# Layer one's local convolution by pairs of heads, with a placing transfer, in a two-layer kernel on one core

## The chip, the core and the metric

One NeuronCore of a Trainium2 chip runs the whole program. The metric is device time in microseconds of that core, the median of several runs. Engines run their own instruction streams and meet only at semaphores: TensorE (PE; PEld is its weight load), VectorE (DVE), ScalarE (ACT), GpSimd (POOL) and SyncE (SP, which here only issues DMAs).

## The reference

16 batches of 1024 tokens and 256 features pass through two layers. Layer zero (a retention with an MLP, then a mixture of experts) is not touched. Layer one is a local dynamic convolution and an MLP. Its convolution, cut to what matters (16 heads of 16 features, a window of 31 tokens):

```python
avg = jnp.cumsum(x, axis=1) / jnp.arange(1, l + 1)[None, :, None]
ci = avg.reshape(b, l, H, d).transpose(0, 2, 1, 3).reshape(b * H, l, d)
pc = ci @ W_pe + b_pe
energy = stt + jax.nn.sigmoid(pc[..., K:]) * pc[..., :K]
w = jax.nn.softmax(energy, axis=-1)              # one kernel of 31 weights for each token and head
for kk in range(K):
    out = out + w[:, :, kk:kk + 1] * padded[:, kk:kk + l, :]
v = conv_loc @ W_fc.T + residual                 # conv_loc: out with the heads side by side
v = (v - mu) / jnp.sqrt(var + EPS) * gamma + beta
```

Around it stand x + ga * v, layer norms with a scale and shift by batch, and an MLP with ReLU (256 to 1024 to 256).

## The kernel before

Layer one runs from about 1941 us to the end of the span. It goes over 16 batches, each cut in 16 slots of a plan. In every slot PE does one slice of the MLP: `l1_expand` (L2294, six matmuls, 512 columns each) and `l1_contract` (L2308, twelve matmuls of 256 columns), of an earlier batch. Between them it does the attention of the current batch: `turn_in` and `turn_mid` (transposes, L130), `kernel_product` (the energies, L2239 and L2244), `window_turn` (transposes, L130), `convolve` (L2265) and `mix` (L2274, L2276).

The order on each engine is written out by the tables `PLACES_D` (batches 2 to 15) and `STARTS_D` (batches 0 and 1): each step has a place in slots, `order_d` turns the places into a plan, all batches' plans are merged by place (batch b starts at slot 16 b) and every engine walks the merged list `t.steps` and issues its own part of each step, in that order. `BANKS_D` says how long a step keeps a PSUM bank; `timed_banks` hands out the banks by it. One batch in the middle of the layer is 16 slots on every engine.

The convolution in blocks of TT = 96 tokens, 11 in a batch (NT), 176 in all:

- `softmax`: DVE makes the 31 weights of each token and head (tile w), and SP writes them to a matrix in DRAM, `bands`, along its diagonals (L1877).
- `load_band`: SP reads the block's matrix back as `bandT` [128 input tokens, 96 output tokens, 16 heads] (L1847, two transfers). The heads are innermost, so one head's 96 columns stand 16 elements (64 bytes) apart.
- `window_turn`: PE turns 128 tokens of the averages, and ACT copies them to `window` (L2022), which has for every pair of heads two 32-column stationary tiles, each with one head's 16 columns and 16 columns of zeros (set once by POOL, L1954 and L1955).
- `convolve`: for each half of the features (k), for odd and even, for four column groups g of 32, one matmul with a 32-column stationary tile and 96 moving columns of bandT. The four g write to partitions 32g to 32g + 31. The odd matmul adds to the even one in PSUM, which the zeros make right. That is 16 matmul calls in a block; each fp32 call stands as two weight loads and two matmuls in the trace, so 32 of each. ACT copies 128x192 to `convT` (L2030), a circle of 384 tokens.
- `mix`: for each chunk of 128 tokens (8 in a batch), transposes of h3T and the product of convT with W_fc, into one bank.

POOL does `join` (moe rows times a gain row, L1935), `add_row` (L1943), the roots and the sum of `energies` (L1962). DVE needs that sum for `energies` (L2139, L2141) after it has made `gated` (L2133). `join` and `add_row` work on half a batch (four chunks, 128x1024) at a time.

## Time and profile before

| | us |
|---|---|
| three runs, median | 3465.27 |
| lowest, highest | 3462.51, 3465.64 |
| the profiled execution's own time | 3466.14 |
| its span | 3464.3 |

```profile
span 3464.3 us, 67597 instructions
PE 3307.4 (95%) x25168; PEld 2785.4 (80%) x25168; DVE 2606.8 (75%) x6172; ACT 2076.2 (60%) x4055; POOL 1269.7 (37%) x1073
PE   7999999999996999999999469999999999999999
DVE  5877887788777865555554578888888888888884
ACT  4677777777765555655665345555555555555554
POOL 1333333332331366666665332333333332322320
PEclk8999999999998999999999689999999999999999
PE 87%; DVE 6%; ACT 2%; DMA 2%; issue 1%; SPq 1%; POOL 1%; POOLq 0%; DVEq 0%; ACTq 0%
```

The second line gives each engine's busy time, its share of the span and its instructions. The digit rows cut the span in 40 slices of 87 us (9 is 90% or more busy); layer one is slices 23 to 40. PEclk is the granted TensorE clock in tenths of full speed. The last line is the chain of work that ended last, followed back and summed by engine.

### The profile page before, as it was taken

To read this page: it belongs to the slowest core of one execution; us is meant where nothing else is said; L and a number is where in the kernel's file an instruction comes from. 1 tells how busy PE (TensorE), PEld (TensorE's weight loads), DVE (VectorE), ACT (ScalarE), POOL (GpSimd) and SP (SyncE) were. 2 spreads that over 40 slices of the span, in tenths; PEclk is the share of its full clock that TensorE was granted. 3 is DMA by queue.
4 is the path that set the end of the run, shared out by engine and by line. 5 is a ranking of instruction groups with operands and counts; after the bars stand their busy time and mean duration, and the time that the engine had idled before them with its cause. 6 is when DMAs were issued, how large, how long until landed. Compare 5 with 4: busy or idle time off the path is not lost.

```text
span 3464.3 us, 67597 instructions
## 1 busy us (share of the span) xinstructions
PE 3307.4 (95%) x25168; PEld 2785.4 (80%) x25168; DVE 2606.8 (75%) x6172; ACT 2076.2 (60%) x4055; POOL 1269.7 (37%) x1073
## 2 busy tenths in 40 slices
PE   7999999999996999999999469999999999999999
PEld 4888888888885799999999347888888888888888
DVE  5877887788777865555554578888888888888884
ACT  4677777777765555655665345555555555555554
POOL 1333333332331366666665332333333332322320
PEclk8999999999998999999999689999999999999999
DMA  5332233222212344444444465555655555655541
GB/s 180 102 114 90 93 114 108 80 64 80 75 45 80 87 115 103 96 104 109 105 97 86 86 132 113 113 127 127 129 125 127 120 123 126 130 125 128 128 102 41
DMA packets 746021, 366.38 MB, mean 106 GB/s; under 512 B 551278, under 2 KB 696246, under 8 KB 745558
## 3 DMA queue, kind: packets, MB, share of 16 engines
q1 hardware_dynamic: 717278, 319.57, 36.4%
q0 software_dynamic: 28416, 42.49, 6.6%
q8 instruction: 201, 3.29, 0.4%
q14 instruction: 126, 1.03, 0.1%
HBM read 224.93 MB, written 135.99 MB: 104 GB/s over the span
## 4 chain that ended last, share of the span: by engine, by line
PE 87%; DVE 6%; ACT 2%; DMA 2%; issue 1%; SPq 1%; POOL 1%; POOLq 0%; DVEq 0%; ACTq 0%
PE bank L2294 10%; PE bank L853 10%; PE bank L1612 10%; PE bank L2308 10%; PE bank L1596 10%; PE bank L833 10%; PE bank L2265 7%; PE bank L130 5%; PE bank L810 3%; PE bank L2244 3%; PE bank L2276 3%; PE bank L2239 1%; ACT sides L1140 1%; PE bank L818 1%; PE bank L846 1%
## 5 line engine op out<-in xcount | busy, mean ns | idle before, releaser
L1492 DVE TENSOR_TENSOR hidden_low<-bank,hidden_high 128x512 fp32r<-128x512 f32 x256 | 176.2, 689 | 263.0 <-ACT hidden_high L1193 262.8
L609 ACT ACTIVATE bank<-bank,b 128x512 f32<-128x512 f32 x256 | 172.7, 675 | 282.2 <-PE bank L833 281.9
L1186 ACT ACTIVATE bank<-bank,fc_bias 128x512 f32<-128x512 f32 x256 | 169.5, 662 | 263.5 <-PE bank L1596 263.5
L853 PE MATMUL bank<-w_high,gT_low 128*128 128x256 f32 x1024 | 309.8, 303 | 2.9 <-DVE gT_low L725 2.9
L2052 ACT ACTIVATE bank<-bank,l_b 128x512 f32<-128x512 f32 x256 | 168.9, 660 | 238.8 <-PE bank L2294 238.8
L2308 PE MATMUL bank<-l_w_high,l_hidden_low 128*128 128x256 f32 x1024 | 307.6, 300 | 0.0
L2265 PE MATMUL bank<-bandT,window 128*32 128x96 f32 x5632 | 271.2, 345 | 22.4 <-DMA bandT<-bands 20.2
L853 PE MATMUL bank<-w_low,gT_high 128*128 128x256 f32 x1024 | 289.4, 283 | 0.0
L853 PE MATMUL bank<-w_high,gT_high 128*128 128x256 f32 x1024 | 289.4, 283 | 0.0
L2308 PE MATMUL bank<-l_w_low,l_hidden_high 128*128 128x256 f32 x1024 | 286.0, 279 | 0.0
L2308 PE MATMUL bank<-l_w_high,l_hidden_high 128*128 128x256 f32 x1024 | 285.5, 279 | 0.0
L2265 PEld LDWEIGHTS bank<-bandT,window 128*32 128x32 f32 x5632 | 187.8, 124 | 90.3 <-issue 46.0
L725 DVE TENSOR_TENSOR gT_low<-bank,gT_high 128x512 fp32r<-128x512 f32 x256 | 172.9, 685 | 113.4 <-ACT gT_high L616 113.4
L1962 POOL TENSOR_TENSOR energies<-energies,energy 128x496 f32<-128x496 f32 x128 | 162.0, 1266 | 209.3 <-DVE energies L2133 209.3
L1106 POOL DMA_INDIRECT moe_output<-ys,idx x128 | 212.3, 1659 | 70.5 <-issue 55.1
L2294 PE MATMUL bank<-h4T_high,l_w_low 128*128 128x512 f32 x512 | 223.2, 436 | 6.8 <-DVE l_v L2166 6.7
L853 PEld LDWEIGHTS bank<-w_high,gT_low 128*128 128x128 f32 x1024 | 194.8, 190 | 24.0 <-issue 13.1
L2308 PEld LDWEIGHTS bank<-l_w_high,l_hidden_low 128*128 128x128 f32 x1024 | 192.6, 188 | 23.4 <-issue 18.9
L833 PE MATMUL bank<-hT_high,w_low 128*128 128x512 f32 x512 | 204.2, 399 | 2.3 <-POOL hT_low L536 2.3
L853 PEld LDWEIGHTS bank<-w_low,gT_high 128*128 128x128 f32 x1024 | 195.5, 191 | 12.0 <-issue 7.2
L833 PE MATMUL bank<-hT_low,w_high 128*128 128x512 f32 x512 | 203.7, 398 | 0.0
L2294 PE MATMUL bank<-h4T_high,l_w_high 128*128 128x512 f32 x512 | 203.0, 396 | 0.0
(372 smaller groups left out, 10709.3 us busy)
## 6 DMA issues: line engine op xcount, KB each, us to landing
bandT<-bands SPq DMA_DIRECT2D x352, 240.0 KB, 3.7
fc_full<-in_L_ffn_fc_wT SPq DMA_DIRECT2D x32, 1024.0 KB, 5.5
bands<-zeros SPq DMA_DIRECT2D x22, 768.0 KB, 8.6
x<-in_L_attn_x SPq DMA_DIRECT2D x32, 512.0 KB, 6.3
moe_output<-zeros SPq DMA_DIRECT2D x32, 512.0 KB, 7.1
x_after_retention<-x SPq DMA_DIRECT2D x32, 512.0 KB, 2.9
moe_input_and_gates<-xn SPq DMA_DIRECT2D x32, 512.0 KB, 7.7
moe<-moe_output SPq DMA_DIRECT2D x32, 512.0 KB, 7.4
```

What stands on the lines that cost most here:

```text
L130: t = pe.transpose(bank[:, i * rows:(i + 1) * rows], source(i), ident[0:rows, 0:rows])
L609: e.activation(bank[:, :], bank[:, :], ACT.Gelu_apprx_tanh, bias=t.b1[:, f:f + 1]).then_inc(s("g_full"), 1)
L725: v.tensor_tensor(t.gT.low[:, f % SLICES, :], K.banks[t.bank["expand", i, f, 0]][:, :], t.gT.high[:, f % SLICES, :], ALU.subtract).then_in ...
L833: m = pe.matmul(bank[:, :], w, h, start=k + j == 0, stop=k == KD - 1 and j == 2)
L853: m = pe.matmul(out, x, w, start=False, stop=f == KF - 1 and j == 2 and c % 2 == 1)
L1106: e.indirect_dma_start(K.moe_dram, bass.IndirectOffsetOnAxis(ap=t.idx[i % 4][:, n:n + 1], axis=0), t.ys[i % 2][:, n, :], None, compute_op= ...
L1492: v.tensor_tensor(t.hidden.low[:, n % SLICES, :], K.banks[t.bank["expand", i, f, 0]][:, :], t.hidden.high[:, n % SLICES, :], ALU.subtract) ...
L1596: m = pe.matmul(bank[:, :], w, y, start=k + j == 0, stop=k == KD - 1 and j == 2)
L1612: p = pe.matmul(y_chunk(K, ch), y, w, start=first and j == 0, stop=f == KF - 1 and j == 2 and ch % 2 == 1)
L2265: m = pe.matmul(bank[32 * g:32 * (g + 1), k * TT:(k + 1) * TT], t.window[n % 2][:, pair, odd, :], t.bandT[n % 2][:, :, g // 2 * H // 2 + k ...
L2294: m = pe.matmul(bank[:, :], w, x, start=k + j == 0, stop=k == KD - 1 and j == 2)
L2308: p = pe.matmul(K.banks[6 + ch // 2][:, left:left + D], x, w, start=False, stop=f == KF - 1 and j == 2 and ch % 2 == 1)
```

## The change

- `window` has one 32-column tile for a pair of heads instead of two with zeros; its columns alternate between the two heads (d, q). ACT's copy L2022 writes with a step of two. The zeroing by POOL and its event go.
- `convolve` has one matmul for a pair of heads, k and g as before: 8 calls instead of 16. The moving side is bandT's columns of both heads, 96 x 2 = 192 columns, pairs of neighbouring elements that stand 64 bytes apart. Each row of the product then holds its own head's result in every second column; the other columns are the other head's weights on this head's features and are not used.
- ACT takes the product with two copies: all 128 rows of the odd columns to a new tile `odd_heads`, all rows of the even columns to convT (128x192 each). A new step `place_odd` issues one DMA from ACT's queue that writes the odd rows of `odd_heads` over those of convT: 64 partitions, two runs of 384 bytes each for a full block.
- `mix` waits for the placing transfers of the last two blocks that it reads. Two blocks later, ACT waits for the transfer before it writes `odd_heads` again. The rows of W_fc are put into the same alternating order on the host.
- `join` and `add_row` become four steps of one chunk each (128x256). The semaphores `gained` and `x2r` count chunks, and all who wait for them do the same.
- All places of layer one and the times in `BANKS_D` are new.

```diff
-    t.window = K.ring(ctx, "window", 2, [P, H // 2, 2, 2 * t.HD])
+    t.window = K.ring(ctx, "window", 2, [P, H // 2, 2 * t.HD])
+    t.odd = K.ring(ctx, "odd_heads", 2, [P, KD, TT])
@@ pool
-            for k, cs in enumerate(pieces_of(n, HC)):
-                e.wait_ge(s("shared"), halves_done(n) if n else k + 1)
-                e.tensor_tensor(t.moe[n % 2][:, cs, :], t.moe[n % 2][:, cs, :], t.row_in[:, :].unsqueeze(1).to_broadcast([P, cs.stop - cs.start, D]),
-                                ALU.mult).then_inc(s("gained"), 1)
+            e.wait_ge(s("shared"), halves_done(n) if n else k // 2 + 1)
+            e.tensor_tensor(t.moe[n % 2][:, k, :], t.moe[n % 2][:, k, :], t.row_in[:, :], ALU.mult).then_inc(s("gained"), 1)
...
-            e.tensor_tensor(x2[:, :, :], x2[:, :, :], t.row_bias[:, :].unsqueeze(1).to_broadcast([P, HC, D]), ALU.add).then_inc(s("x2r"), 1)
+            e.tensor_tensor(x2[:, k, :], x2[:, k, :], t.row_bias[:, :], ALU.add).then_inc(s("x2r"), 1)
@@ scalar
-            e.copy(out, src).then_inc(s("window"), 1)
+            e.copy(t.window[n % 2][:, :, :].rearrange("p a (d q) -> p a q d", q=2),
+                   K.banks[t.bank["window_turn", b, *args, 0]][:, 0:D].rearrange("p (a q d) -> p a q d", q=2, d=t.HD)).then_inc(s("window"), 1)
...
+            if n >= 2:
+                e.wait_ge(*K.later(f"odd_placed{n % 2}", 16 * (n // 2)))
+            heads = K.banks[t.bank["convolve", b, i, 0]][:, 0:2 * KD * TT].rearrange("p (k t q) -> p k t q", k=KD, q=2)
+            e.copy(t.odd[n % 2][:, :, 0:size], heads[:, :, 0:size, 1])
             if before:
                 e.wait_ge(s("mixed"), before)
-            e.copy(t.convT[:, :, place:place + size],
-                   K.banks[t.bank["convolve", b, i, 0]][:, 0:KD * TT].rearrange("p (k t) -> p k t", k=KD)[:, :, 0:size]).then_inc(s("convT"), 1)
+            e.copy(t.convT[:, :, place:place + size], heads[:, :, 0:size, 0]).then_inc(s("conv_taken"), 1)
+        elif name == "place_odd":
+            (i,) = args
+            n, size, place = b * NT + i, min(TT, K.S - i * TT), i * TT % t.CIRCLE
+            e.wait_ge(s("conv_taken"), n + 1)
+            e.dma_start(t.convT[1::2, :, place:place + size], t.odd[n % 2][1::2, :, 0:size]).then_inc(K.later(f"odd_placed{n % 2}")[0], 16)
@@ tensor
             for k in range(KD):
-                for odd in range(2):
-                    for g in range(4):
-                        pair = 4 * k + g
-                        m = pe.matmul(bank[32 * g:32 * (g + 1), k * TT:(k + 1) * TT], t.window[n % 2][:, pair, odd, :],
-                                      t.bandT[n % 2][:, :, g // 2 * H // 2 + k * t.HR + g % 2 * 2 + odd], start=odd == 0, stop=odd == 1)
+                for g in range(4):
+                    first = g // 2 * H // 2 + k * t.HR + g % 2 * 2
+                    out = bank[32 * g:32 * (g + 1), 2 * k * TT:2 * (k + 1) * TT].rearrange("p (t q) -> p t q", q=2)
+                    m = pe.matmul(out, t.window[n % 2][:, 4 * k + g, :], t.bandT[n % 2][:, :, first:first + 2], start=True, stop=True)
...
-            pe.wait_ge(s("convT"), NT * b + -(-(ch + 1) * P // TT))
+            last = NT * b + -(-(ch + 1) * P // TT) - 1
+            for n in range(max(last - 1, 0), last + 1):
+                pe.wait_ge(*K.later(f"odd_placed{n % 2}", 16 * (n // 2 + 1)))
```

The lines of `PLACES_D` of which the prediction speaks, before and after:

```diff
-    "kernel_product": (10.8, 12.8, 14.85, 16.8, 18.8, 20.8, 22.79, 24.8), "gated": (10.8, 12.8, 14.61, 16.8, 18.82, 20.8, 22.8, 24.8),
-    "energies": (11.61, 13.56, 15.61, 17.61, 19.47, 21.61, 23.61, 24.94),
-    "convolve": (16.82, 18.13, 19.59, 21.03, 22.48, 23.93, 25.38, 26.83, 28.28, 29.73, 31.18),
-    "mix": (19.06, 20.4, 21.9, 24.8, 26.2, 27.7, 30.6, 31.43), "center_mid": (19, 20.4, 21.9, 24.8, 26.21, 27.7, 30.6, 32),
+    "kernel_product": (10.8, 13.01, 14.91, 16.8, 18.93, 20.89, 22.77, 24.74),
+    "gated": (10.69, 12.36, 14.84, 16.96, 18.61, 20.81, 22.64, 24.58),
+    "energies": (11.36, 13.53, 15.74, 17.73, 19.27, 21.35, 23.56, 25.52),
+    "convolve": (16.97, 18.08, 19.67, 21.03, 22.22, 23.95, 25.04, 26.82, 28.62, 29.73, 31.18),
+    "place_odd": (17.09, 18.19, 19.9, 21.15, 22.42, 24.02, 25.25, 27.02, 28.74, 29.98, 31.32),
+    "mix": (19.15, 20.49, 22.1, 24.89, 26.55, 27.9, 31.23, 32.35),
```

## Rows read from the trace of the kernel before

**Rows 1.** Busy time by stretch: middle batches, then the layer's start.

```profile
core 0: us, PE busy (x) PEld busy (x) DVE busy (x) ACT busy (x) POOL busy (x), PEclk, DMA share, GB/s
2456.00:2546.00 90.00, 89.52 (x828) 73.26 (x826) 77.85 (x159) 52.34 (x107) 27.46 (x22) 1.00 0.58 125
...
2726.00:2816.00 90.00, 89.52 (x828) 73.49 (x826) 77.86 (x159) 52.54 (x106) 27.48 (x22) 1.00 0.59 125
...
1980.00:2070.00 90.00, 57.35 (x604) 41.10 (x604) 72.50 (x137) 38.47 (x80) 27.25 (x20) 0.78 0.67 137
```

**Rows 2.** Waits from 2456 to 2816 us (four batches): total, times, longest.

```profile
DVE top L2139 <- POOL energies L1962: 25.4, 24, 2.0
DVE energies L2133 <- ACT l_th L2002: 9.2, 12, 1.7
DVE total L2146 <- ACT energies L2010: 5.5, 8, 0.7
PE bank L2294 <- DVE l_v L2166: 1.9, 4, 0.5
```

**Rows 3.** Timeline of PE, 2700 to 2712 us: start, duration, instructions merged.

```profile
2700.73 1.53 PE L2265 MATMUL bank<-bandT,window 128*32 128x96 f32 x32
2702.19 0.50 PE L2294 MATMUL bank<-h4T_high,l_w_low 128*128 128x512 f32 x1
...
2703.69 0.28 PE L2308 MATMUL bank<-l_w_high,l_hidden_low 128*128 128x256 f32 x1
...
2705.19 0.49 PE L2239 MATMUL bank<-pe_bias,l_ones 64*128 64x496 f32 x2
...
2706.45 0.44 PE L130 MATMUL bank<-ident,avgT 128*128 128x128 f32 x2
2706.72 0.38 PE L2274 MATMUL bank<-ident,h3T 128*128 128x128 f32 x2
...
2710.72 0.74 PE L2304 MATMUL bank<-out_bias,l_ones 128*128 128x512 f32 x2
2711.30 0.28 PE L2308 MATMUL bank<-l_w_high,l_hidden_low 128*128 128x256 f32 x1
```

**Rows 4.** Lines from 2456 to 2816 us, shapes apart: busy, mean ns.

```profile
L2265 PE MATMUL bank<-bandT,window 128*32 128x96 f32 x1408 | 67.8, 344 | 0.0
L1962 POOL TENSOR_TENSOR energies<-energies,energy 128x496 f32<-128x496 f32 x32 | 40.1, 1254 | 39.7 <-DVE energies L2133 39.7
L1935 POOL TENSOR_TENSOR moe<-moe,row_in 128x1024 f32<-128x1024 f32 x8 | 20.5, 2565 | 39.2 <-ACT moe L1975 39.2
L2030 ACT COPY convT<-bank 128x192 f32<-128x192 f32 (+1 forms) x44 | 13.8, 314 | 22.1 <-PE bank L2265 22.1
```

**Rows 5.** Timeline of PE around the router's product in layer zero.

```profile
149.60 0.64 PE L867 MATMUL bank<-xnT,w_router 128*32 128x128 f32 x16
```

**Rows 6.** The router's product, all 512: duration min/median/max.

```profile
L867 PE MATMUL bank<-xnT,w_router x512: 272/273/421, 149.6 to 1074.2; 128*32 128x128 f32 x171
```

**Rows 7.** A convolution at low clock: PE's timeline, then its stretch.

```profile
1984.10 1.57 PE L2265 MATMUL bank<-bandT,window 128*32 128x96 f32 x32 [1.72 <-DMA bandT<-bands]
...
1984.00:1986.00 2.00, 1.57 (x32) 1.21 (x32) 1.97 (x3) 0.86 (x2) 0.00 (x0) 0.50 0.72 140
```

**Rows 8.** Timeline of ACT behind the convolution of Rows 3.

```profile
2702.34 0.32 ACT L2030 COPY convT<-bank 128x192 f32<-128x192 f32 x1 [0.69 <-PE bank L2265]
...
2704.59 0.59 ACT L2059 CAST l_hidden_high<-bank 128x512 fp32r<-128x512 f32 x1
```

**Rows 9.** Timeline of SP's queue: how long it is busy with an issue.

```profile
2702.33 0.77 SPq L1847 DMA_DIRECT2D bandT<-bands  x2
2705.90 0.32 SPq L1877 DMA_DIRECT2D bands<-w  x1
```

**Rows 10.** DMA issues: KB each, median us from issue to landing.

```profile
bands<-w SPq DMA_DIRECT2D x79, 62.0 KB, 4.2
...
ranks<-rank SPq DMA_DIRECT2D x4, 256.0 KB, 2.3
...
rows_layer<-rows SPq DMA_DIRECT2D x2, 64.0 KB, 1.9
...
x_after_retention<-x SPq DMA_DIRECT2D x32, 512.0 KB, 2.9
```

**Rows 11.** Waits from 1941 to 2070 us, the start of the layer.

```profile
PE bank L130 <- ACT moe L1982: 30.0, 2, 24.4
...
PE bank L2265 <- DMA bandT<-bands: 19.9, 6, 7.0
```

119 lines of the change are left out of this document (61 added, 58 removed).

## The prediction, made before the change was run

> **What bounds the kernel now.** I read the busy time by stretch first. In the middle of layer one a batch takes 90.0 us, and PE is busy 89.5 of them at full granted clock, while DVE is busy 77.9, ACT 52.3 and POOL 27.5 [rows 1]. Busy time of PE alone proves little, so the waits come next: over four batches PE waits 1.9 us for another engine, all else on the list are others waiting [rows 2]. PE's own stream therefore sets the 90 us, and what shortens that stream shortens the batch until DVE, with 77.9 us of work, becomes the limit. The chain that ended last gives PE 87%, which agrees. The layer's first 130 us are different: from 1980 to 2070 us PE is busy only 57 of 90 us, with waits of 30.0 us on ACT's moe and 19.9 us on bandT [rows 1, 11]. There latency sets the pace, and less work on PE brings little.
>
> **The convolution on PE.** A block of 32 matmuls lasts 1.53 us, one of them 0.344 us [rows 3, 4]. The four column groups run side by side, so 32 matmuls are eight steps of four, and the last start comes 1.53 - 0.34 = 1.19 us after the first: 1.19 / 7 = 0.17 us a step. The next line starts 1.46 us after the block's start. After the change there are 16 matmuls, four steps, each with 192 columns instead of 96. Everything hangs on the length of such a step.
>
> The router's product has the same form, 128x32 stationary, four column groups, fp32, but its moving columns stand side by side. Its 16 matmuls of 128 columns last 0.64 us at 0.273 each: (0.64 - 0.27) / 3 = 0.12 us a step [rows 5, 6]. So a step with four loads and four matmuls can be done in 0.12 us, and 128 columns cost less than the convolution's 96. Neither loads nor instructions set the 0.17 us, then, and by the router's 0.96 ns a column 96 columns would take 0.09. What differs is the 64-byte spacing of bandT's columns. A second row agrees: at the low level of the granted clock (0.50, 1.2 GHz) the block takes 1.57 us instead of 1.53 [rows 7, 3]; a step bound by the array would have doubled. I conclude that each separate place in bandT costs 0.17 / 96 = 1.8 ns whatever stands there. Then 96 places with a pair in each cost 0.17 us a step again, and 192 columns at the router's rate cost 192 x 0.96 = 0.18 us. The two ways agree on 0.17 to 0.18.
>
> The Trainium skill has two rules here that contradict each other. "TensorE: Matmul & The Clock Gate" (What happens when you issue a matmul) says that throughput is purely the number of columns streamed; 16 x 96 and 8 x 192 are the same number, and by that rule the saving is nil. "SBUF — State Buffer" (the note on cachelines) says that fp32 reads need two hits in a 16-byte line for full rate; by that rule pairs run at full rate and the step stays. The rows above speak for the second, and only for single elements; no row shows a pair.
>
> So a block gets four steps shorter: 4 x 0.17 = 0.68 us, or 7.5 us for the 11 blocks of a batch. Bounds: nothing, if a step of 192 takes 0.34 us, and 0.68 if it stays. In 15 batches (165 blocks) PE loses 165 x 0.68 = 112 us. In batch 0, where PE waits anyway, half the blocks run at the low clock, where 192 columns cannot be faster than the 1.2 GHz allows; I take nothing there.
>
> **ACT.** It gets a second copy, 0.31 us, and an issue of a DMA. No DMA is issued by ACT in this trace; SP's queue is busy 0.32 to 0.39 us with one [rows 4, 9]. That is 11 x (0.31 + 0.35) = 7.3 us a batch on an engine with 52.3 of 90 us: 59.6 of some 83. It stays second to DVE. A copy with a step of two on either side may be slower; at twice the 0.31 for both, another 7 us would still fit. Every copy, split or rectifier of ACT behind it comes up to 0.65 us later, and slots of the MLP have more than that between their parts (ACT now waits for PE before most of them).
>
> **The placing transfer and mix.** Before, mix could go 0.15 + 0.32 us after the convolution (PE's next line starts at 2702.19, the copy runs 2702.34 to 2702.66) [rows 3, 8]. Now: 0.15, two copies 0.63, in some blocks one `l1_split` of 0.59 ahead of the issue by the places (19.67 convolve, split of the slot, 19.9 place_odd), then the transfer. It moves 48 KB within SBUF, which no row shows. Nearest are the 64 KB and 256 KB issues with 1.9 and 2.3 us; 4.2 us for 62 KB into `bands` is the far end, with its many small runs, and 2.9 for 512 KB lies between [rows 10]. I take 2.3, near the small ones with some queueing. The sum is 3.1 us, 3.7 with the split, 5.6 at worst.
>
> What covers it is PE's work between convolution and mix, from the places: PE has an expand 1.50, a contract 1.50, an energies product 1.26 and a turn of the window 0.27 [rows 3]. Before, the chunk mixed at 27.7 had one contract and one turn behind its convolution (26.83), 1.8 us. In the new places the shortest are the chunks mixed at 20.49 and 27.9, behind the convolutions at 19.67 and 26.82: each has an expand, a turn and the first contract of a half between, which carries the output bias (0.58 us) [rows 3]: 3.8 us. The others have 4.1 us and more. The margin of the two is 0.1 to 0.7 us, so small delays on ACT or in the transfer will show; I charge 0.6 us a batch (ends: 0 and, at 5.6 us, 2 x 1.8 + 3 x 1.2 = 7 us). Behind a waiting mix stands the whole of PE, so each such wait counts in full.
>
> **POOL and DVE.** POOL's own time is the same but for a little overhead. Cutting a 2.57 us join into four lets the energies' sum (1.25 us) go after a chunk [rows 4]. DVE now waits 25.4 / 4 = 6.4 us a batch for that sum [rows 2], because in most chunks only one `l1_low` of some 0.7 us lies between `gated` and `energies` (places 10.8 and 11.61, 20.8 and 21.61). In the new places most chunks have more between (10.69 to 11.36 holds residual_mid and stats_x3; 12.36 to 13.53 an add_in besides), so I expect 1 to 2 us a batch to be left. That matters: DVE's 77.9 plus all its present waits of 12.1 is 90.0, and without relief DVE could not keep up with a batch of 82.5. With 2 us left, and 1.4 us for the exponentials' wait (5.5 / 4), it needs 81.3. That fits, with 1 us to spare, so some friction is to be expected; I charge 0.4 us a batch.
>
> **Start and end.** In batch 0 a mix has hardly cover, and five of eight could wait 2 us for the placing, partly inside the wait for bandT that follows: +3 us, between 0 and +10. POOL's zeroing that falls away is under 2 us at a time when PE waits for other things: nothing. The end behind the last convolution is the MLP's and stays.
>
> **Sum.** Profiled execution 3466.1 - 112 + 15 x (0.6 + 0.4) + 3 = 3372. It stands 0.9 us above the median of three, so 3371. A middle batch would be 90.0 - 7.5 + 1.0 = 83.5 us.
>
> **Rivals.**
> - Pairs cost double (slower). If each fp32 element read outside a contiguous run costs 1.8 ns, a step of 192 takes 0.34 us, PE's stream is as long as before, and the friction and the start remain: 3465 + 18 = 3483; with mix at its worse end, more. For it: the same number of elements is read, and no row shows a pair. Against: the element next door arrives with the same access if the limit is the place and not the element. The change turns slower once a step is above about 0.17 + 0.17 x (112 - 18) / 112 = 0.31 us. Chance 0.09.
> - DVE becomes the bound. If its waits for POOL and ACT stay at 7 to 9 us a batch instead of 3.4, a batch takes 85 to 87 us, and the time is 3465 - 15 x (3.0 to 5.0) + 3, some 3393 to 3423. For it: 94% load on an engine that waits in order. Against: the longer cover between its steps. Chance 0.13.
> - The placing transfer is late. With DMA engines busy 0.58 of the time [rows 1] it could land after 4.2 us; 7 us a batch would cost nearly all the gain. More likely 1.5 to 3.5 us a batch are lost beyond my charge: 3395 to 3425. Chance 0.05.
>
> **Chances and range.** The forecast (3371, its own range 3347 to 3392) has 0.73; the low end is the full 119 us with no friction. The range goes to 3422 to take in most of the next two. About 0.2% (7 us) is what a measurement tells here. Faster 0.89, same 0.02, slower 0.09.
>
> **What would show it.** L2265 has 2816 matmuls; a block lasts about 0.85 us (3 x 0.17 and one duration) instead of 1.53. If it lasts 1.3 or more, the first rival holds. A middle batch is 83 to 84 us with PE over 98% busy; PE waits for the placing DMA in front of L2274 show the third rival; PE waiting for l_hidden_low or bank readers on DVE, and DVE over 95% busy, the second. DVE's wait for L1962 should fall under 2 us a batch. ACT's busy time rises to about 56 us a batch, issues not counted.

## The result

| | us |
|---|---|
| the kernel before, 14 runs beside those of the changed one, median | 3467.65 (3459.63 to 3472.02) |
| the changed kernel, 14 runs, median | 3472.26 (3465.87 to 3481.86) |
| ratio, 95% interval | 1.0017 (1.001 to 1.0025) |
| its profiled execution, and the span of it | 3470.05, 3468.2 |

The prediction was 3371 us. The change brings nothing: it is 0.1 to 0.25% slower. Yet PE has 2816 matmuls less, as was forecast, and 87 us less of busy time, of the 112 us that were forecast.

The head of the profile of the changed kernel, to be read beside that of before:

```profile
span 3468.2 us, 62699 instructions
PE 3220.2 (93%) x22352; PEld 2684.6 (77%) x22352; DVE 2652.3 (76%) x6172; ACT 2109.9 (61%) x4231; POOL 1327.4 (38%) x1262
PE   7999999999996899999999468999999999999999
DVE  5877887788777865555554577999999989998984
PEclk8999999999998999999999779999999999999999
PE 77%; DVE 11%; issue 4%; ACT 4%; DMA 2%; POOL 1%; SPq 1%; another core or an unknown queue 0%; ACTq 0%; DVEq 0%; POOLq 0%
```

PE's part of the chain of work that ended last fell from 87 to 77%, DVE's rose from 6 to 11 and "issue" from 1 to 4. The same stretches as [rows 1]:

```profile
2456.00:2546.00 90.00, 84.30 (x659) 67.43 (x658) 82.26 (x161) 55.05 (x118) 33.24 (x37) 1.00 0.62 135
...
2726.00:2816.00 90.00, 84.97 (x659) 68.42 (x660) 82.25 (x159) 54.88 (x119) 33.21 (x36) 0.98 0.61 131
1980.00:2070.00 90.00, 48.45 (x334) 30.14 (x334) 64.25 (x121) 38.89 (x86) 31.24 (x32) 0.71 0.56 118
```

PE is busy 84.3 of 90 us instead of 89.5, so it now has 5 to 6 us of gaps in each middle batch. DVE is busy 82.3 instead of 77.9, though it has the same instructions in a batch (a small part of this is that 90 us now hold a little more than a batch).

**Where the time went, by batch.** A batch is measured from the first subtraction of `top` of one batch to that of the next (every eighth row of that instruction on DVE). These are the starts of batches 0, 1, 2 and 15, first of before, then of after:

```profile
1962.92 2.10 DVE L2141 TENSOR_TENSOR energies<-energies,top 128x496 f32<-128x496 f32 x1
2038.42 2.11 DVE L2141 TENSOR_TENSOR energies<-energies,top 128x496 f32<-128x496 f32 x1
2128.77 2.16 DVE L2141 TENSOR_TENSOR energies<-energies,top 128x496 f32<-128x496 f32 x1
3298.74 2.15 DVE L2141 TENSOR_TENSOR energies<-energies,top 128x496 f32<-128x496 f32 x1
```
```profile
1970.60 1.16 DVE L2153 TENSOR_TENSOR energies<-energies,top 128x496 f32<-128x496 f32 x1
2055.28 0.68 DVE L2153 TENSOR_TENSOR energies<-energies,top 128x496 f32<-128x496 f32 x1
2147.87 0.67 DVE L2153 TENSOR_TENSOR energies<-energies,top 128x496 f32<-128x496 f32 x1
3309.07 0.68 DVE L2153 TENSOR_TENSOR energies<-energies,top 128x496 f32<-128x496 f32 x1
```

Batch 0 takes 84.7 us instead of 75.5, batch 1 92.6 instead of 90.4, and the thirteen batches 2 to 14 take 89.3 us each instead of 90.0; 83.5 was forecast. The part behind the mark of batch 15 takes 159.2 instead of 165.6 us, 6.4 less: the convolutions of batch 15 lie there. (The mark of batch 0 itself comes 7.7 us later. That can't be put down to the change: in the other kernels with its places the mark lies anywhere from 1960 to 1971 us.)

The experiments are compared by these figures, taken from the same rows of their traces. Some batches hold a stretch at the lower level of TensorE's granted clock (0.50, 1.2 GHz), so the mean of the batches without one is given too, with their number:

| kernel | batch 0 | batch 1 | mean of 2 to 14 | those without low clock | ratio to before |
|---|---|---|---|---|---|
| before | 75.5 | 90.4 | 90.0 | 90.0 (13) | 1 |
| after | 84.7 | 92.6 | 89.3 | 88.5 (10) | 1.0017 |
| e1: convolution alone, old places | 80.6 | 103.0 | 101.8 | none | 1.0568 |
| e2: after, GpSimd by halves | 84.5 | 92.6 | 93.2 | 91.6 (4) | 1.0153 |
| e3: places and chunks alone | 74.5 | 85.2 | 92.4 | 92.4 (11) | 1.008 |
| e4: row addition moved | 85.2 | 91.7 | 91.0 | 90.3 (6) | 1.006 |
| f1: mix doesn't wait | 75.2 | 82.7 | 88.3 | 87.8 (4) | 0.9907 |
| f2: no transfer | 73.8 | 84.8 | 88.5 | 87.9 (2) | 0.9902 |
| f3: light join and row addition | 79.2 | 93.2 | 88.8 | 87.5 (7) | 0.9957 |
| f4: old places, later mix | 81.5 | 97.5 | 94.7 | 95.5 (1) | 1.0212 |
| g1: f2 and f3 together | 71.2 | 82.8 | 85.8 | 85.7 (12) | 0.9781 |
| g2: residual_mid earlier | 82.4 | 91.3 | 92.5 | 88.8 (1) | 1.0095 |
| g3: batch 0's mixes later | 75.5 | 91.0 | 90.6 | 88.4 (5) | 1.0015 |
| g4: f2 with less work on VectorE | 72.3 | 82.4 | 88.3 | 87.5 (4) | 0.9888 |
| h1: gain_out ahead of residual_mid | 81.4 | 92.3 | 90.0 | 87.8 (6) | 0.9997 |
| h2: h1, g3 and more | 75.8 | 90.9 | 95.8 | none | 1.0218 |
| h3: light sum of energies | 83.2 | 92.6 | 88.3 | 87.3 (9) | 0.994 |
| i1: h1, g3, later wait | 75.8 | 91.6 | 89.8 | 87.3 (3) | 0.9972 |

Each row is one profiled execution. How much two executions of the same places can differ is shown by g3, which changes batch 0 alone: its batches 2 to 14 take 90.6 us in the mean, 1.3 more than those of after, yet its batches without low clock take 88.4, after's 88.5. Eight of its thirteen hold such a stretch, three of after's. So a difference of about 1 us between two means of this table isn't read as an effect of order. The medians in us that are compared below with after's 3472.26 stem from different sets of runs, in which the median of before itself lay between 3463.4 and 3467.7; such differences are good to some 5 us.

### The profile page after: what moved, and what is told of

It is laid out like the page before. It is cut to its first block, busy times and chain, and to the rows that moved or that the text cites. A ratio compares the mean times of both kernels' runs of the same rounds, so it can differ in the third digit from the quotient of the medians.

```text
span 3468.2 us, 62699 instructions
## 1 busy us (share of the span) xinstructions
PE 3220.2 (93%) x22352; PEld 2684.6 (77%) x22352; DVE 2652.3 (76%) x6172; ACT 2109.9 (61%) x4231; POOL 1327.4 (38%) x1262
## 4 chain that ended last, share of the span: by engine, by line
PE 77%; DVE 11%; issue 4%; ACT 4%; DMA 2%; POOL 1%; SPq 1%; another core or an unknown queue 0%; ACTq 0%; DVEq 0%; POOLq 0%
PE bank L854 10%; PE bank L1613 10%; PE bank L1597 10%; PE bank L834 10%; PE bank L2321 8%; PE bank L2307 8%; PE bank L131 6%; PE bank L811 3%; PE bank L2277 3%; PE bank L2256 2%; PE bank L2289 2%; DVE more_x L2188 2%; PE bank L2251 1%; DVE l_stats L648 1%; ACT sides L1141 1%
## 5 line engine op out<-in xcount | busy, mean ns | idle before, releaser
L1971 POOL TENSOR_TENSOR energies<-energies,energy 128x496 f32<-128x496 f32 x128 | 180.6, 1411 | 660.6 <-DVE energies L2145 660.5
L1107 POOL DMA_INDIRECT moe_output<-ys,idx x128 | 203.7, 1592 | 70.5 <-issue 55.1
L2307 PE MATMUL bank<-h4T_low,l_w_high 128*128 128x512 f32 x512 | 203.0, 397 | 0.0
L834 PE MATMUL bank<-hT_high,w_high 128*128 128x512 f32 x512 | 200.6, 392 | 0.0
```

Source lines behind the costliest of these rows:

```text
L834: m = pe.matmul(bank[:, :], w, h, start=k + j == 0, stop=k == KD - 1 and j == 2)
L1107: e.indirect_dma_start(K.moe_dram, bass.IndirectOffsetOnAxis(ap=t.idx[i % 4][:, n:n + 1], axis=0), t.ys[i % 2][:, n, :], None, compute_op= ...
L1971: e.tensor_tensor(e1[:, :, :], e1[:, :, :], t.energy[:, :, :], ALU.add).then_inc(s("full_energy"), 1)
L2307: m = pe.matmul(bank[:, :], w, x, start=k + j == 0, stop=k == KD - 1 and j == 2)
```

## What the trace of after shows first

**The convolution did get shorter.** PE's timeline around one block, to be read beside [rows 3], then the line over four batches beside [rows 4]:

```profile
2707.82 0.88 PE L2277 MATMUL bank<-bandT,window 128*32 128x192 f32 x16
2708.63 0.50 PE L2307 MATMUL bank<-h4T_high,l_w_low 128*128 128x512 f32 x1
```
```profile
L2277 PE MATMUL bank<-bandT,window 128*32 128x192 f32 x704 | 38.8, 334 | 0.0
```

The next line starts 0.81 us after the block instead of 1.46: 0.65 us saved a block, 7.2 a batch (0.68 and 7.5 were forecast). One matmul of 192 columns lasts 0.334 us, one of 96 lasted 0.344. PE's stream of a batch is thus 90.0 - 7.2 = 82.8 us. The measured batch is 6.5 us longer: gaps, and in three batches low clock.

**The gaps.** The waits of the same four batches as [rows 2]; the first column after the colon is the total over four:

```profile
PE bank L2317 <- DVE o L2216: 9.1, 4, 2.3
DVE energies L2145 <- ACT l_th L2011: 8.2, 8, 1.8
DVE l_stats L2171 <- PE bank L2289: 7.2, 8, 1.7
PE bank L2287 <- issue: 6.4, 8, 1.7
DVE top L2151 <- POOL energies L1971: 3.1, 4, 0.8
```

DVE's wait for POOL's sum fell from 25.4 to 3.1, 0.8 us a batch, where 1 to 2 were forecast. In its place PE waits 2.3 us in every batch for `o`, the read of a bank of the MLP's output, and 1.6 us in front of `mix` (L2287; 1.9 us a batch over all mixes of batches 2 to 14). Before the first of these waits, DVE and POOL did this:

```profile
2537.62 3.14 DVE L2188 SCALAR_TENSOR_TENSOR more_x<-l_v,l_root_mid,more_x 128x256 f32<-128x256 f32 x4
...
2537.78 1.43 POOL L1971 TENSOR_TENSOR energies<-energies,energy 128x496 f32<-128x496 f32 x1 [8.17 <-DVE energies L2145]
...
2539.17 0.92 POOL L1954 TENSOR_TENSOR more_x<-more_x,row_bias 128x256 f32<-128x256 f32 x1
...
2540.69 1.28 DVE L2216 TENSOR_TENSOR o<-bank,row_out 128x512 f32<-128x512 f32 x2
...
2542.11 0.70 PE L2317 MATMUL bank<-out_bias,l_ones 128*128 128x512 f32 x2 [2.26 <-DVE o L2216]
```

The four instructions of residual_mid (L2188) take 3.14 us; before they take 4 x 0.478 = 1.91. POOL is at work on SBUF for nearly all of that time. One by one the four take 0.48, 1.48, 0.95 and 0.47 us: the two long ones are those that start while one of POOL's two instructions runs, and each ends shortly after it. So the new places did what they were meant to do, but the work put between `gated` and `energies` as cover is slowed by the very sum that it covers. The rows of the lines say how much, over four batches, first of before, then of after:

```profile
L2176 DVE SCALAR_TENSOR_TENSOR more_x<-l_v,l_root_mid,more_x 128x256 f32<-128x256 f32 x24 | 10.0, 478 | 0.0
L2101 DVE TENSOR_TENSOR more_x<-more_x,moe 128x1024 f32<-128x1024 f32 x6 | 7.3, 1216 | 0.0
L2141 DVE TENSOR_TENSOR energies<-energies,top 128x496 f32<-128x496 f32 x32 | 30.8, 964 | 1.1
```
```profile
L1971 POOL TENSOR_TENSOR energies<-energies,energy 128x496 f32<-128x496 f32 x32 | 45.3, 1415 | 160.1 <-DVE energies L2145 160.1
L2188 DVE SCALAR_TENSOR_TENSOR more_x<-l_v,l_root_mid,more_x 128x256 f32<-128x256 f32 x24 | 20.3, 905 | 0.0
L2113 DVE TENSOR_TENSOR more_x<-more_x,moe 128x1024 f32<-128x1024 f32 x6 | 11.4, 1904 | 0.0
L1954 POOL TENSOR_TENSOR more_x<-more_x,row_bias 128x256 f32<-128x256 f32 x26 | 22.7, 884 | 0.0
L2153 DVE TENSOR_TENSOR energies<-energies,top 128x496 f32<-128x496 f32 x33 | 25.6, 776 | 1.1
```

Eight instructions of residual_mid and two of add_in stand in a batch: 8 x 0.43 + 2 x 0.69 = 4.8 us more on DVE, against the 6.4 - 0.8 = 5.6 us of wait that went. The subtraction of `top`, which in before met the long row addition, gave 8 x 0.19 = 1.5 us back. Net, DVE is busy 81.4 us in a batch of after (mean of batches 2 to 14), 3.5 more than the 77.9 of before.

**The start.** One of PE's rows with a wait in front of mix in batch 0; there are five such in it, of 2.3, 2.9, 4.0, 4.2 and 5.8 us, and three in batch 1, of 4.9, 2.4 and 0.9:

```profile
2032.63 0.66 PE L2287 MATMUL bank<-ident,h3T 128*128 128x128 f32 x2 [4.22 <-DMA convT<-odd_heads]
```

## The experiments

First the question which part of the change costs what. In all of them the edit is to the kernel after; where its convolution is taken back or its places are, the text says so.

**e1, convolution alone.** All places of before, `join` and `add_row` by halves:

```diff
-    "place_odd": (17.09, 18.19, 19.9, ...), and all other places of after
+    "place_odd": each convolve + 0.13, and all other places of before
```

> The new convolution with its two copies and the placing transfer, at the places of before (place_odd 0.13 slots behind convolve), join and add_row by halves as before. Theory A (the new places let GpSimd's add_row and join run beside VectorE's residual_mid and add_in, which slows both, and gain_out behind residual_mid holds PE): here the pairing is the old one, residual_mid stays at 0.48 us an instruction, VectorE keeps its 78 us a batch, and the batch falls from 90.0 to about 86: 3400 to 3420 us. Theory B (the placing transfer, 3.0 us from issue to landing, holds mix and with it PE): at the old places only 1.5 to 1.8 us of PE's work lie between convolution and mix for two chunks and 3.2 for three, against a chain of 4.4 us; that is 2 x 2.8 + 3 x 1.2 = 9 us of waits a batch, more than the 7.3 that the convolution gives: 3465 to 3490 us.

Measured: 3661.38 against 3466.64, ratio 1.0568 (1.0551 to 1.0586). The direction was that of the theory which makes mix wait, the size far beyond it. In front of mix PE waits 50.2 us from 2456 to 2816 us, at most 3.6 at a time. Per batch PE's waits in front of its eight mixes sum to 14 us, but a batch is 19 us longer than 82.8: the clock has stretches at its lower level (a mean of 0.95 from 2546 to 2636 us, and one or more in each of batches 2 to 14; before has none after 2130 us). residual_mid takes 0.477 us and add_in 1.216, as before. So the slower DVE instructions do not come from the new convolution, and with the old places PE's waits for the placing transfer are the largest cost.

**e2, halves again, with after's places.**

```diff
-    "join": (4.01, 4.27, 4.41, 4.67, 12.81, 13.04, 13.24, 13.25), "add_row": (11.06, ..., 18.95, ...)
+    "join": (4.67, 13.25), "add_row": (11.06, 18.95), each of half a batch
```

> The changed kernel with join and add_row by halves again (join at its last chunk's place, add_row at its first chunk's). Theory A1 (the cutting into chunks makes GpSimd and VectorE take turns at each other's cost): GpSimd's two operations return to 2.4 to 2.6 us a half, residual_mid to near 0.48, and the time falls by 2 to 3 us a batch: 3425 to 3440. Theory A2 (the places bring them together, whatever the grain): the same total overlap, residual_mid stays near 0.9 us in the mean, the time stays within 0.3% of the changed kernel, 3460 to 3480.

Measured: 3518.73, ratio 1.0153 (1.0136 to 1.017), outside of both. The subtraction of `top` (two SBUF inputs, now at times beside a join or row addition of 2.4 us) takes 1.36 us in the mean instead of 0.78. The chunks are worth some 47 us at these places.

**e3, places and chunks alone.** The convolution of before, no transfer:

```diff
-    one matmul for a pair of heads, two copies, place_odd
+    two matmuls for a pair of heads, one copy (as before); chunks and places of after
```

> The old convolution (32 matmuls, no placing) at the new places and with the chunks. Theory A: VectorE is slowed here as well (residual_mid near 0.9 us), gain_out late, and PE, whose stream is 90 us again, pays some waits on top: 92 to 94 us a batch, 3490 to 3530 us. Theory B: without the placing transfer nothing new holds PE, 90.0 us a batch and 3465 to 3475.

Measured: 3495.7, ratio 1.008 (1.0063 to 1.0097), as theory A says. An instruction of residual_mid takes 0.924 us here: the slowing of DVE comes with the places. Alone they cost 2.4 us in a middle batch, of which PE's wait for `o` is 1.7; batches 0 and 1 gain by them.

**e4, row addition away from residual_mid.**

```diff
-    "add_row": (11.06, 11.42, 12.11, 12.51, 18.95, 19.78, 20.18, 20.49), "load_bias_row": 4.46
+    "add_row": (16.55, 16.56, 16.57, 16.58, 22.35, 22.36, 22.37, 22.38), "load_bias_row": 7.0
```

> The changed kernel with add_row of batches 2 to 15 at other places (16.55 and 22.35, chunks kept, load_bias_row at 7.0), away from residual_mid and where GpSimd has nothing else. Theory A: residual_mid returns from 0.91 to near 0.48 us (1.7 us a half), gain_out comes earlier and PE no longer waits 2.3 us for it: 3 to 4 us a batch less over 14 batches, 3415 to 3430 us. Theory B: PE's waits stay, the time stays within 0.3% of the changed kernel.

Measured: 3486.19, ratio 1.006 (1.0043 to 1.0077): slower than after, a miss. residual_mid fell only to 0.726 us, and add_row, which now met other DVE work, rose to 1.051, h4T_low to 0.950 (0.683 elsewhere). `h4T_low` too has two inputs in SBUF. The contention moved; PE's wait in front of mix rose from 1.6 to 2.9 us a batch (over the same four batches), and six batches without low clock take 90.3 us against after's 88.5.

**f1 and f2, what the transfer costs.** f1 keeps it but sends it to rows that nobody reads; f2 leaves it out. In both mix waits for the copies only.

```diff
-            for n in range(max(last - 1, 0), last + 1):
-                pe.wait_ge(*K.later(f"odd_placed{n % 2}", 16 * (n // 2 + 1)))
+            pe.wait_ge(s("conv_taken"), NT * b + -(-(ch + 1) * P // TT))
-            e.dma_start(t.convT[1::2, :, place:place + size], t.odd[n % 2][1::2, :, 0:size])
+            e.dma_start(t.odd[n % 2][0::2, :, 0:size], t.odd[n % 2][1::2, :, 0:size])    # f1; nothing in f2
```

> The changed kernel, but the transfer goes from the odd rows of odd_heads to its even rows, which nothing reads, and mix waits only for ACT's copies (as before). Leaves out the placing of the odd heads, so their share of the convolution is not in the product. ACT still issues each transfer (0.60 us). Theory B (waiting for the transfer is the loss): batch 0 falls from 84.7 to about 75 us and the middle batches from 89.3 (mean of batches 2 to 14) by the 1.7 us that PE waits for it and what follows from it, to 86: 3410 to 3425 us. Theory A (contention of GpSimd and VectorE and the order of VectorE's steps hold the middle batches): only batches 0 and 1 gain, about 17 us, 3450 to 3458 us. Theory C (the issue on ACT is the loss): little is gained here, and the rest in the run without any transfer.

> The changed kernel without the transfer, its issue and its waits; both copies stay. Leaves out the placing of the odd heads. Beside the run with the unread transfer this gives the price of 11 issues of 0.60 us a batch on ACT. Theory C: ACT (70.8 us of instruction time a batch against 60.3 before) comes late for the rectifiers and splits, and without the 6.6 us the batch falls 1 to 3 us below that of the other run. Theories A and B: within 0.3% of it.

Measured: 3430.77 and 3430.94 against 3463.52, ratios 0.9907 (0.989 to 0.9923) and 0.9902 (0.9886 to 0.9919). That lies between the ranges of theories B (3410 to 3425) and A (3450 to 3458), outside both; theory C is refuted. The two kernels are the same within what these runs tell, so no cost of the issue on ACT or of the load on the DMA engines is seen: what the transfer costs is PE's waiting for it. Of the 41 us between after and these two, batches 0 and 1 hold 84.7 + 92.6 - 75.2 - 82.7 = 19.4, the thirteen middle ones 13 x 1.0 = 13. Without the transfer a middle batch is still 88.5, 5.7 us above PE's stream.

**f3, GpSimd's join and row addition made light.** They work on 4 of 256 columns:

```diff
-            e.tensor_tensor(t.moe[n % 2][:, k, :], t.moe[n % 2][:, k, :], t.row_in[:, :], ALU.mult)
+            e.tensor_tensor(t.moe[n % 2][:, k, 0:4], t.moe[n % 2][:, k, 0:4], t.row_in[:, 0:4], ALU.mult)
```

> The changed kernel with GpSimd's join and add_row on 4 columns a chunk instead of 256. Leaves out most of two additions and products by rows. Theory A: residual_mid returns to 0.48 us an instruction and add_in to 1.22, VectorE's instructions fall by 4.5 to 5 us a batch, and a batch from 89.3 to 85 or 86: 3405 to 3425 us. Theory B: VectorE is faster, the batch stays above 88 us, since PE waits for the transfer: 3455 to 3470 us.

Measured: 3449.14, ratio 0.9957 (0.9942 to 0.9971), outside both. One instruction of residual_mid takes 0.726 us instead of 0.905, not the expected 0.48, and add_in 1.904 as in after. DVE's wait for POOL's sum is 3.1 us over four batches, as in after, so a shorter queue on POOL is not what DVE gained by.

**h3, the sum of the energies made light.** One of 31 columns of each head:

```diff
-            e.tensor_tensor(e1[:, :, :], e1[:, :, :], t.energy[:, :, :], ALU.add)
+            e.tensor_tensor(e1[:, :, 0:1], e1[:, :, 0:1], t.energy[:, :, 0:1], ALU.add)
```

> The changed kernel with GpSimd's sum of the energies on 1 of 31 columns a head. Leaves out most of that addition. If VectorE's instructions with two SBUF inputs are held by a GpSimd instruction that reads SBUF, add_in returns from 1.90 to 1.22 us, and residual_mid falls by about 0.18 us (the part that stayed away in the run with light join and add_row), though both kinds of instruction touch nothing of each other's data. If the stretch is from join and add_row, or from VectorE's own order, both stay as they are. Time: 1 to 3 us a batch less, 3425 to 3455 us.

Measured: 3443.55, ratio 0.994 (0.9924 to 0.9957).

```profile
L2188 DVE SCALAR_TENSOR_TENSOR more_x<-l_v,l_root_mid,more_x 128x256 f32<-128x256 f32 x24 | 14.4, 658 | 0.0
L1971 POOL TENSOR_TENSOR energies<-energies,energy 128x16 f32<-128x16 f32 x33 | 13.3, 402 | 182.1 <-DVE energies L2145 182.1
...
L2113 DVE TENSOR_TENSOR more_x<-more_x,moe 128x1024 f32<-128x1024 f32 x6 | 7.3, 1216 | 0.0
```

The time is as expected. With the sum all but gone, add_in is back at 1.216, its time in before, with no other change. f3 and h3 together account for the whole of residual_mid: 0.905 - 0.726 = 0.179 from the row addition, 0.905 - 0.658 = 0.247 from the sum, and 0.905 - 0.179 - 0.247 = 0.479, the 0.478 of before. That POOL's instructions lengthen DVE's is thus shown, not only argued. The other way round the effect is smaller: the sum takes 1.415 us instead of 1.254.

The Trainium skill says of this, in "SBUF — State Buffer" (SBUF: two separate sides), that a DVE operation with two SBUF inputs and a GpSimd operation that reads SBUF share a pair of ports that one of them holds for a whole instruction. The rows agree in which operations are slowed: the ones with a PSUM input, such as `l_hidden_low` at 0.68 us, keep their time. They agree with the holding too: the residual_mid of 1.48 us above starts 0.23 us after the sum and ends 0.28 us behind it.

**g1, f2 and f3 together.**

> The changed kernel without the transfer and with join and add_row on 4 columns, the two relieving edits together. Leaves out the placing of the odd heads and most of two GpSimd operations. Each alone left the middle batches at 88.5 and 88.8 us, from 89.3. Theory D (each relieved one of two queues that hold PE in turn, VectorE's length and the transfer, so that the other took over): together the batch falls to 84 to 85.5 us, 3370 to 3390 us. Theory E (what holds PE at 88 is neither: the order of the steps on VectorE and ACT in the new places): no more than the sum of both single gains, 87.5 to 88 us and about 3410 to 3415 us.

Measured: 3386.95, ratio 0.9781 (0.9765 to 0.9797). Alone the two edits bring 41 and 23 us, together 85, so each was hidden in part while the other cost stood. That is the time of theory D, though its reason, the length of VectorE's queue, is refuted by the next run. A middle batch takes 85.8 us; only one of the thirteen holds low clock, eleven in f2 and six in f3. Still PE waits 1.9 us in each batch for `o`; residual_mid takes 0.727 here, slowed by the sum.

**g4, is it DVE's amount of work?** f2, with add_in and the result's addition on 4 of 256 columns, which takes 3 us a batch from DVE:

```diff
-            v.tensor_tensor(x2[:, cs, :], x2[:, cs, :], t.moe[n % 2][:, cs, :], ALU.add)
+            v.tensor_tensor(x2[:, cs, 0:4], x2[:, cs, 0:4], t.moe[n % 2][:, cs, 0:4], ALU.add)
```

> The changed kernel without the transfer, and VectorE's add_in and result on 4 columns a chunk (6.2 us of VectorE's instructions a batch). Leaves out the placing of the odd heads and most of the two additions. Theory D: VectorE's queue is the limit of the middle batches, which fall from 88.5 to 84 or 85 us: 3375 to 3395 us. Theory E: less than 2 us a batch, 3405 us or more.

Measured: 3423.22, ratio 0.9888 (0.9871 to 0.9904); a middle batch 88.3 beside f2's 88.5, as theory E says. DVE is busy 80.4 of 90 us instead of 83.2. So it isn't the sum of DVE's work that holds the batch. That it is what stands in front of the few instructions for which PE waits is the reading that is left.

**The single waits taken away.** Four kernels move steps within after's order:

```diff
 g2: "residual_mid": (27.08, 34.63)  ->  (27.08, 33.4)
 g3: STARTS_D[0] "mix": (18.82, 20.45, 22.09, 24.94, 26.33, ...)  ->  (19.7, 21.9, 22.78, 25.9, 27.4, ...)
 h1: "gain_out": (42.31, 50.68)  ->  (42.31, 50.62)
 h2: g3 and h1; every place_odd right behind its convolve; "mix": 24.89, 26.55 -> 25.3, 27.0; "norm_in": 8.96 -> 9.045
```

> The changed kernel with residual_mid of the second half at 33.4 instead of 34.63 for batches 2 to 15: VectorE does it behind gated, ahead of the exponents' steps, and gain_out, for which PE waits 2.3 us a batch before its output bias, no longer stands behind it. Theory A: that wait falls under 0.8 us and a batch by 1 to 2 us, 3440 to 3455 us. Theory E2 (VectorE is full, so the time only moves to the next step that PE waits for): within 0.3% of the changed kernel.

Measured: 3497.81, ratio 1.0095 (1.0078 to 1.0112), slower than after by more than either theory allows. The wait for `o` is gone, but PE now waits 2.1 us a batch for avgT (L2192, 8.2 over four) and twice as long in front of mix (13.8 over four instead of 6.4).

> The changed kernel with the first five mixes of batch 0 0.7 to 1.1 slots later, behind the next energies product and turn of the window, so that PE has work while the transfer runs. Theory B: batch 0 takes 84.7 us instead of 75 only because the whole of PE stands behind a mix that waits 2.5 to 6 us; it falls by 4 to 8 us, 3460 to 3466 us. If batch 0 is bound by something else, it stays within 2 us.

Measured: 3467.01 (10 runs), ratio 1.0015 (0.9999 to 1.003). Batch 0 went from 84.7 to 75.5 us, the time of before: 9.2 us, where 4 to 8 were expected. The start's cost in batch 0 is the place of those mixes. The time, 1 us above the expected range, is only 5 us better than after's. In this profile the middle batches are longer by the low clock that eight of them hold, though their places are unchanged.

> The changed kernel with gain_out of the second half ahead of residual_mid instead of behind it in batches 2 to 15 (50.62 for 50.68). Theory A: PE's wait of 2.3 us for the output banks goes, with it the low-clock windows that follow it; 2 to 3 us a batch less, 3430 to 3445 us. Theory E2 (PE's waits are taken up by the next step that VectorE is late with): within 0.3% of the changed kernel, as residual_early showed for the opposite move.

Measured: 3462.78 (10 runs), ratio 0.9997 (0.9987 to 1.0007). That is theory E2. The wait for `o` went, and the gaps in front of mix rose from 1.9 to 3.7 us a batch. The six batches without low clock take 87.8 us, 0.7 less than after's, but seven instead of three now hold a stretch of it.

> The changed kernel with all repairs by places alone: gain_out first, the later mixes of batch 0, every place_odd directly behind its convolve in ACT's order, norm_in of the first half behind the seventh convolution's copies, the fourth and fifth mix 0.4 slots later. Theory B with A: batch 0 near 75 us, mix's waits in the middle batches from 2.3 to under 0.5 us, a middle batch at 85 to 86.5 us: 3405 to 3430 us, faster than both kernels. If low clock and VectorE's order keep a batch at 88: 3450 to 3465 us.

Measured: 3538.18, ratio 1.0218 (1.0201 to 1.0235), a miss. PE now waits 13.6 us for moe and 10.5 for avgT over four batches, and DVE 39.6 us, at most 9.1 at a time, for the product of mix.

**f4, the old places with a mix that comes later** (1.25 slots behind the convolution, by halves):

```diff
-    "mix": (19.15, 20.49, ...), all other places of after
+    "mix": each 1.25 behind its last convolve, root_mid, residual_mid and stats_x3 behind it, all other places of before
```

> The new convolution at the places of before with halves (the run e1_conv_alone, 103 us a batch), but every mix 1.25 slots behind its last convolution instead of 0.25 to 0.93, and the steps behind it moved by what that asks. Theory B: PE's 14 us a batch of waits at mix go, the batch falls to 84 to 87 us: 3385 to 3430 us. If something else in these places had held PE (the VectorE waits of 6.4 us a batch for GpSimd's sum), it stays above 88 us.

Measured: 3538.45, ratio 1.0212 (1.0195 to 1.0229): 123 us better than e1 but a miss. DVE waits 5 us a batch for the sum and 6 for `l_th`, and mix still waits 3.6. Of the two ways tried to fit the transfer into the old places, neither pays.

**i1, the best of it together.** g3 and h1, and PE's wait for the transfer put behind the two transposes of h3T, which don't need it:

```diff
+            for n in range(max(last - 1, 0), last + 1):
+                pe.wait_ge(*K.later(f"odd_placed{n % 2}", 16 * (n // 2 + 1)))
             for k in range(KD):
                 m = pe.matmul(bank[:, 0:D], t.convT[:, k, place:place + P], ...
```

> The changed kernel with the later mixes of batch 0, gain_out first, and mix's wait for the transfer behind its two transposes, which do not need it. If the gains add (5 us from the start, 5 to 9 from gain_out, up to 0.22 us at each waiting mix): 3450 to 3458 us, some 0.2 to 0.4% faster than the kernel before. If the middle batches take it up again: 3460 to 3467 us.

Measured: 3459.11 (12 runs), ratio 0.9972 (0.996 to 0.9984). It is faster than before by 0.3% and than after by 0.4%, and it is the fastest kernel here that does all of the work. It is still 88 us from the 3371. It lies between the ranges of its two expectations. What it gained is the start: batch 0 takes 75.8 us, a middle batch 89.8, no less than in after. The three middle batches without low clock take 87.3 us, the ten with it 90.6.

## Why the prediction was wrong

**The convolution: right.** 0.65 us a block measured, 0.68 forecast, by the step length from the router's rows [rows 3, 5, 6]. A block of four steps lasts 0.88 us, one matmul 0.33, so a step takes (0.88 - 0.33) / 3 = 0.18 us for 192 columns, and took 0.17 for 96 single ones. The rival by which pairs cost double is refuted. Why PE's busy time fell by 87 us and not by 112 isn't resolved in full. Low clock is a part of it: the batch of after that holds two stretches of it has PE busy 85.6 us, a batch without one 82.9 (rows below), and from 1980 to 2070 us the mean granted clock is 0.71 instead of 0.78.

**"That fits, with 1 us to spare": the step that failed.** DVE's time in a batch was put at 77.9 + 2 + 1.4 = 81.3 us, and two things were wrong in it. First, the wait for `l_th`, 9.2 / 4 = 2.3 us a batch in [rows 2], was left out without a reason. With it the sum is 83.6, and nothing was to spare in a batch of 82.5. In after that wait is still 2.1 us, but the waits for the sum and for the exponentials fell to 0.8 each; all three are 3.6 us where 3.4 were assumed, so luck made this error harmless. Second, and this is what failed: the wait for POOL fell even further than forecast, but its removal was priced at what the cover costs when it runs alone. residual_mid and add_in read two operands from SBUF, and beside POOL's sum and row addition they take 0.905 instead of 0.478 and 1.904 instead of 1.216 us. Of 5.6 us of wait, 4.8 came back as work, and 1.5 were won at `top`: DVE is busy 81.4 us instead of 77.9 in a batch, and with its waits comes to 85.0 (by itself that sum isn't the bound either, as g4 shows). Charged for all friction were 0.4 us a batch, 6 us in all. Taking the sum's part of the slowing away brings 29 us (h3), the other part with the join 23 (f3).

The slowing accounts for only part of PE's wait for `o`: that wait is still 1.6 us with the sum made light and 1.7 with the join and row addition made light, and 0 where gain_out stands ahead of residual_mid (h1). The rest of it is the order of the steps.

The trace of before held a warning. The instructions of the subtraction of `top`, also with two SBUF inputs, as shortest, median and longest in ns:

```profile
L2141 DVE TENSOR_TENSOR energies<-energies,top x128: 674/675/2165, 1962.9 to 3373.1; 128x496 f32<-128x496 f32 x128
```

One form, three times as long in some places as in others. I read only the waits and not the spread of durations. The rival "DVE becomes the bound", at 0.13, pointed at the right engine, but its price (85 to 87 us a batch, 3393 to 3423 us) was too low, and its condition did not hold: DVE's waits for POOL and ACT did not stay at 7 to 9 us, they fell to (3.1 + 8.2 + 3.0) / 4 = 3.6. As a bound by amount of work it is refuted by g4.

**The placing transfer: mis-sized.** The issues and the transfer itself:

```profile
convT<-odd_heads ACTq DMA_DIRECT2D x40, 48.0 KB, 3.0
```

```profile
2570.37 2.07 ACT L1991 ACTIVATE moe<-x,l_center_in,l_root_in 128x256 f32<-128x256 f32 x4
2572.34 0.30 ACT L2035 COPY odd_heads<-bank 128x192 f32<-128x192 f32 x1
2572.54 0.32 ACT L2038 COPY convT<-bank 128x192 f32<-128x192 f32 x1
2573.25 1.45 ACT L2000 ACTIVATE h3T<-bank,mod_columns 128x512 f32<-128x512 f32 x2 [0.39 <-PE bank L131]
2575.03 0.60 ACTq L2043 DMA_DIRECT2D convT<-odd_heads  x1
```

It lands after 3.0 us (2.3 forecast, 1.9 to 4.2 the bounds); ACT's queue is busy 0.60 us with one issue (0.35 forecast). In a middle batch ACT's order adds about as much as the transfer's own excess: this issue comes 2.2 us behind its copy, since turn_in's copies to h3T stand between, and the copies themselves are late by norm_in's four. The fourth and fifth mix of a batch wait 0.9 and 0.7 us on average, and not the second and sixth, which I had named and whose PE cover was the shortest (0.1 us each). All mixes together wait 1.9 us a batch; 0.6 was charged, 7 was the far end. I had counted PE's cover and a split, not what else stands ahead of a copy on ACT. That ACT's order is the reason is read from this timeline; h2 removes the waits of those two mixes, but it changes five things at once. What the transfer costs in time is shown: 41 us with the start (f1, f2), where 15 x 0.6 + 3 = 12 were charged.

**The start: mis-sized.** +3 us, 0 to 10, were forecast for batch 0, from five waits of 2 us. It takes 9.2 us more. Its mixes waited 19.1 us, 2.3 to 5.8 each. That more than half is hidden was right: PE's waits in front of the convolution and of the energies product are 18.2 and 15.1 us in batch 0 of f1, 11.7 and 8.0 in that of after. The waits were too short in the forecast, not the hiding too generous. Batch 1 wasn't in that term at all: it waits 8.2 us in front of mix and gains nothing, and with batch 0 it is 19.4 us above f1.

**The clock: not in the prediction.** Between 2130 and 3400 us before has no stretch with a granted clock below 1.00. After has four, f2 twelve, g2 nineteen, g1 two, e1 thirty-one; nearly all last 3.4 us, at the lower level (1.2 GHz). A middle batch of after without one, the batch with two, and one with one, cut at the marks:

```profile
2679.70:2768.60 88.90, 82.93 (x652) 66.22 (x651) 81.55 (x158) 54.69 (x117) 32.11 (x34) 1.00 0.61 132
2768.60:2862.10 93.50, 85.63 (x652) 68.47 (x651) 81.32 (x158) 54.56 (x117) 31.40 (x34) 0.96 0.58 126
3127.60:3220.20 92.60, 84.19 (x645) 66.99 (x647) 81.46 (x159) 54.78 (x117) 32.03 (x35) 0.98 0.60 127
```

The three batches of after that hold one or two take 90.2, 92.6 and 93.5 us, the ten others 88.5 on average: 10.9 us in all, or 0.8 of the 89.3 - 83.5 = 5.8 that a middle batch is over the forecast. In f2, where eleven of thirteen middle batches hold one, the two without take 86.9 and 88.9 and the others 87.8 to 89.5. So a stretch need not cost more than the 3.4 - 1.7 = 1.7 us of half speed, an estimate, and the rest of the 4 to 5 us in two batches of after would be waiting that stands beside it. In g3, h1 and i1 the batches with one are 3.2 to 4.1 us longer than those without, and there are seven to ten of them. So the clock is a rival to the order of the steps wherever their middle batches are compared with after's. Which of the two, waiting and low clock, brings the other wasn't separated. What is shown is that before, whose PE hardly waits, has none.

**What the parts sum to.** Forecast for a middle batch 83.5. Measured 89.3. Taking the transfer away gives 88.5, the join and row addition 88.8, both 85.8. The 3.0 us from there to 82.8 hold PE's waits for `o` (1.9) and `moe` (0.7). In time, the two edits together give back 85 of the 101 us between forecast and result; the last 16 are open, as is which order would save them without leaving work out: each attempt to move one wait (e4, g2, h1, h2) made another. A kernel without any two-input DVE work beside POOL was not tried.

## To carry to other kernels

Before you call work on VectorE a free cover for a GpSimd operation, look at where its operands lie: if both inputs are in SBUF and GpSimd reads SBUF too, the trace of a neighbour with the same form tells what the meeting costs. Here PE was 99% busy before the change, and the order of each other engine had been fitted to its pace. In such a kernel a 7 us saving on PE needs slack on every engine that feeds it, and a transfer added between two PE steps must be counted from the last instruction ahead of the copy that starts it. Try such a change in parts: here the new step alone cost 195 us at the old places, and the places alone 29. And compare single batches beside the mean: with one profile of each kernel, low clock in a few batches looks like an effect of the order.

## What the runs showed of the hardware

- With four column groups side by side, a moving fp32 operand of 96 single elements 64 bytes apart takes PE 0.17 us a step; 96 pairs of neighbours at the same spacing, 192 columns, take 0.18. By the rule of the Trainium skill that throughput is purely the number of columns ("TensorE: Matmul & The Clock Gate", What happens when you issue a matmul) the block would have kept its 1.46 us; it took 0.81. The Trainium skill's other rule, that fp32 reads need two hits in a 16-byte line for full rate ("SBUF — State Buffer", Specifications (TRN2)), fits.
- A DMA of 64 rows of two 384-byte runs within SBUF lands after 3.0 us, and its issue holds ACT's queue 0.60 us; SP's issues take 0.32 to 0.39 [rows 9].
- VectorE with two SBUF inputs beside GpSimd: 1.216 to 1.904 us (128x1024), 0.478 to 0.905 (128x256); with one of the two GpSimd operations made light, residual_mid takes 0.726 and 0.658, and the two parts add up. GpSimd's sum itself goes from 1.254 to 1.415.
- In the kernel before, where PE's longest wait from 2130 to 3400 us is 0.5 us, the granted clock has no stretch at its lower level in that time. The kernels of this case in which PE waits some 2 us at a time have between two and thirty-one, most of 3.4 us. Which waits bring one on, no run here shows.
